# Causal attention scored on four row groups of the tensor engine, and layer norms that add their squares in halves before the variance matmul

## What is computed

```python
def _layernorm(x, axis=-1, eps=1e-05):
    m = jnp.mean(x, axis=axis, keepdims=True)
    v = jnp.var(x, axis=axis, keepdims=True)
    return (x - m) / jnp.sqrt(v + eps)
```

## Time and profile before

| | us |
|---|---|
| median of 3 runs | 2788.03 (2782.67 to 2789.25) |
| the profiled execution | 2787.26 |
| its span | 2785.5 |
| PE busy | 2124.0 (76%) |
| DVE busy | 1838.7 (66%) |
| ACT busy | 1340.7 (48%) |
| POOL busy | 1012.5 (36%) |
| mean granted TensorE clock | 0.896 |

### The profile page before, as it was taken

One profiled execution on the slowest core, in us unless ns is written; L12 is line 12 of the kernel. 1 busy time (PEld: TensorE's weight loads), 2 busy tenths in 40 slices (PEclk: granted clock), 3 DMA queues, 4 the chain that ended last, 5 costly groups with the idle time before them and its releaser, 6 DMA issues. The chain is left out here.

```text
span 2785.5 us, 34483 instructions
## 1 busy us (share of the span) xinstructions
PE 2124.0 (76%) x12315; PEld 1350.6 (48%) x12315; DVE 1838.7 (66%) x2425; ACT 1340.7 (48%) x2235; POOL 1012.5 (36%) x651
## 2 busy tenths in 40 slices
PE   2787666045698888988856999998896677689996
PEld 0455553012566666666634777775443233244442
DVE  4359883966677777777723554554353697899975
ACT  0013223552676677666632322323454685556655
POOL 1014532305246777777623333334110000443430
PEclk7998777576899999999968999999998898899998
DMA  3225555004448999999760000002132540000001
GB/s 137 60 97 193 192 196 201 0 0 137 166 154 245 260 255 249 255 261 257 181 234 0 1 1 0 0 0 106 46 113 83 204 152 1 0 1 1 1 1 61
DMA packets 123676, 313.50 MB, mean 113 GB/s; under 512 B 29569, under 2 KB 49537, under 8 KB 119810
## 3 DMA queue, kind: packets, MB, share of 16 engines
q1 hardware_dynamic: 102466, 260.69, 26.5%
q0 software_dynamic: 21056, 50.84, 9.2%
HBM read 219.59 MB, written 92.68 MB: 112 GB/s over the span
## 5 line engine op out<-in xcount | busy, mean ns | idle before, releaser
L1407 DVE SCALAR_TENSOR_TENSOR x_part<-x_group,x_scale,x_part 128x256 f32<-128x256 f32 x660 | 288.0, 477 | 144.7 <-ACT x_part L1349 136.9
L1296 PE MATMUL x_group<-x_xt,x_gu 128*128 128x256 f16 x2640 | 347.1, 275 | 1.8 <-DVE x_xt L1399 0.9
L1349 ACT ACTIVATE x_part<-x_group,x_scale 128x256 f32<-128x256 f32 x660 | 276.2, 471 | 123.1 <-PE x_group L1296 117.2
L1262 POOL TENSOR_TENSOR x_part<-x_part 128x512 f32<-128x512 f32 x165 | 235.3, 1430 | 197.2 <-DVE x_part L1407 197.2
L1296 PEld LDWEIGHTS x_group<-x_xt,x_gu 128*128 128x128 fp8e4 x2640 | 237.6, 98 | 85.7 <-issue 31.7
L1633 POOL TENSOR_TENSOR c_pt<-c_pt,const_tables 128x256 f32<-128x256 f32 x128 | 127.8, 1019 | 280.6 <-ACT c_pt L1741 280.3
L1313 PE MATMUL x_y_ps<-x_d_hi,x_h_hi 128*128 128x512 f32 x330 | 160.2, 485 | 68.8 <-DVE x_h_lo L1420 66.8
L2420 POOL TENSOR_TENSOR f_part<-f_part 128x1024 f32<-128x1024 f32 x44 | 120.4, 2735 | 187.9 <-DVE f_part L2447 187.9
L155 PE MATMUL mean_n<-residual,const_tables 128*128 128x512 f32 x160 | 80.0, 652 | 137.4 <-PEq L734 103.5
L2318 PE MATMUL f_group<-f_x_hi,f_raw 128*128 128x512 f16 x352 | 138.9, 395 | 32.3 <-DVE f_part L2447 24.9
L1253 POOL DMA_INDIRECT mixed_rows<-x_y,moe_rows x94 | 150.1, 1597 | 31.1 <-issue 20.8
(11 more groups left out here) (335 smaller groups left out, 5290.9 us busy)
## 6 DMA issues: line engine op xcount, KB each, us to landing
x_d_hi<-down_hi SPq DMA_DIRECT2D x50, 768.0 KB, 5.6
x_d_lo<-down_lo SPq DMA_DIRECT2D x50, 768.0 KB, 5.9
x_gu<-codes_gu SPq DMA_DIRECT2D x50, 384.0 KB, 5.8
p_w<-d_s SPq DMA_DIRECT2D x17, 768.0 KB, 7.5
down_hi<-p_hi SPq DMA_DIRECT2D x17, 768.0 KB, 3.9
down_lo<-p_lo SPq DMA_DIRECT2D x17, 768.0 KB, 6.2
aux<-ct SPq DMA_DIRECT2D x2, 4096.0 KB, 17.0
cross_values<-y_v_out SPq DMA_DIRECT2D x16, 512.0 KB, 3.0
```

The lines of the kernel that those rows point to most:

```text
L1262: pool.tensor_tensor(x[:, 0, :, :], x[:, 0, :, :], x[:, 1, :, :], ALU.add).then_inc(summed, 1)
L1296: mm = pe.matmul(group_ps[s % 2][:, q, :], codes[:, q, col:col + P], xt[u][:, k, q, :], start=k == 0, stop=k == 1)
L1349: act.activation(part[n % PARTS][:, q, o % 2, :], group_ps[s % 2][:, q, :], ACT.Copy, scale=scale[v][:, o, q:q + 1]).then_inc(ev_act, 1)
L1407: dve.scalar_tensor_tensor(x, group_ps[s % 2][:, 2 + q, :], scale[v][:, o, 2 + q:3 + q], x, ALU.mult, ALU.add).then_inc(ev_dve, 1)
```

## The change

**In the layer norm** VectorE gets a new step, `pair`: it adds chunks 2 and 3 of the squares onto chunks 0 and 1, in place. The variance then takes two matmuls a tile in place of four, and waits for `pair`. VectorE's queue is written out anew; TensorE's and ScalarE's keep their order.

**In the causal attention** q and k keep their layout and `spread` is gone: head j of a chunk lies on rows 32j to 32j+31, and the four heads of a chunk are scored by matmuls on four row groups, each into a PSUM bank of its own (`s_ps` takes four banks, and there is one of it). The 512 ** -0.5 moves into the exponential, which takes four heads at once (1536 columns), as does the mask; `pt` is a ring of three such groups. The squares of q and k are added on VectorE (`add_squares`) and summed by one matmul of 512 columns. The order of work is written out, without a loop, and the value projection reads the residual, not a copy of it.

```diff
             def var(t):
-                pe.wait_ge(squares_ready, base + t + 1)
+                pe.wait_ge(paired, base + t + 1)
                 if t >= 2:
                     pe.wait_ge(ln_ready, base + t - 1)
-                for c in range(C):
+                for c in range(C // 2):
                     mm = pe.matmul(var_ps[t % 2][:, :], g.const("mean"), squares[t % 2][:, c, :],
-                                   start=c == 0, stop=c == C - 1)
+                                   start=c == 0, stop=c == C // 2 - 1)
                 mm.then_inc(var_ready, 1)
 
             mean(0)
@@ -178,18 +177,36 @@
                 dve.tensor_tensor(centred[t][:, :, :], tile(src, t), bc(mean_ps[t % 2][:, :], 1, [P, C, TT]),
                                   ALU.subtract).then_inc(centred_ready, 1)
 
+            def pair(t):
+                dve.wait_ge(squares_ready, base + t + 1)
+                x = squares[t % 2]
+                dve.tensor_tensor(x[:, 0:2, :], x[:, 0:2, :], x[:, 2:4, :], ALU.add).then_inc(paired, 1)
+
+            def scale(t):
+                dve.wait_ge(rs_ready, base + t + 1)
+                dve.tensor_tensor(tile(dst, t), centred[t][:, :, :], bc(rs[t % 2][:, :], 1, [P, C, TT]),
+                                  ALU.mult).then_inc(normed, 1)
+
             if fill_vector is not None:
                 fill_vector(dve, 0)
             centre(0)
             centre(1)
-            for t in range(NT):
-                if t + 2 < NT:
-                    centre(t + 2)
-                if fill_vector is not None and t >= 1:
-                    fill_vector(dve, t)
-                dve.wait_ge(rs_ready, base + t + 1)
-                dve.tensor_tensor(tile(dst, t), centred[t][:, :, :], bc(rs[t % 2][:, :], 1, [P, C, TT]),
-                                  ALU.mult).then_inc(normed, 1)
+            pair(0)
+            centre(2)
+            pair(1)
+            if fill_vector is not None:
+                fill_vector(dve, 1)
+            scale(0)
+            centre(3)
+            pair(2)
+            if fill_vector is not None:
+                fill_vector(dve, 2)
+            scale(1)
+            pair(3)
+            if fill_vector is not None:
+                fill_vector(dve, 3)
+            scale(2)
+            scale(3)
 
         @block.scalar
...
-        xb = sb("xb", [P, C, S])
         q_raw, k_raw = sb("q_raw", [P, C, S]), sb("k_raw", [P, C, S])
-        sq, sk = sb("sq", [P, C, S]), sb("sk", [P, C, S])
+        squares = sb("squares", [P, 2, C, S])
+        pairs, sums = sb("pairs", [P, 2, 2, S]), sb("sums", [P, 2, S])
         nrm = sb("nrm", [P, 2, S])
-        q_sb = [sb(f"q{i}", [P, C, S]) for i in range(2)]
-        k_sb = sb("k", [P, C, S])
-        kp = [sb(f"kp{i}", [P, 4, S]) for i in range(2)]
-        v_sb = [sb(f"v{i}", [P, 2, D]) for i in range(2)]
-        pt = [sb(f"pt{i}", [P, 3, P]) for i in range(RING)]
-        at = [sb(f"at{i}", [P, C, S]) for i in range(2)]
-        out_ps, den_ps, work = ps("out_ps", [P, C, S]), ps("den_ps", [P, C, S]), ps("work", [P, C, S])
+        q_sb, k_sb = two("q", [P, C, S]), two("k", [P, C, S])
+        v_sb = two("v", [P, 2, D])
+        pt = [sb(f"pt{i}", [P, 4, 3, P]) for i in range(PT_RING)]
+        at = two("at", [P, C, S])
+        s_ps = ps("s", [P, 4, 4, P])
+        out_ps, den_ps = ps("out_ps", [P, 2, S]), ps("den_ps", [P, 2, S])
+        work = ps("work", [P, C, S])
         work_v = work[:, :, :].rearrange("p (k n) s -> p k (n s)", k=2)
-        s_ps = [ps(f"s{i}", [P, 3, P]) for i in range(2)]
...
-            def score(b, i, h):
-                c, j = h // 4, h % 4
-                if j == 0:
-                    pe.wait_ge(kp_ready, C * b + c + 1)
-                pe.wait_ge(exped, H1 * b + h + 1)
-                pe.matmul(s_ps[h % 2][:, 0:2, :], kp[c % 2][:, j, 0:P], q_sb[i][:, c, :], start=True, stop=True)
-                pe.matmul(s_ps[h % 2][:, 2, :], kp[c % 2][:, j, P:S], q_sb[i][:, c, P:S], start=True, stop=True)\
-                  .then_inc(s_done, 1)
...
+            def norms(b):
+                pe.wait_ge(v_read, b + 1)
+                pe.wait_ge(summed, b + 1)
+                pe.matmul(work[:, 2:4, :], g.const("ones"), sums[:, :, :], start=True, stop=True).then_inc(norm_done, 1)
+
...
+            def score(b, c):
+                n = GROUPS * b + c
+                if c == 0:
+                    pe.wait_ge(qk_ready, 2 * b + 2)
+                if n >= 1:
+                    pe.wait_ge(exped, n)
+                for k in range(2):
+                    for j in range(4):
+                        r = slice(32 * j, 32 * j + 32)
+                        out = s_ps[:, j, 0:2, :] if k == 0 else s_ps[:, j, 2, :]
+                        mm = pe.matmul(out, k_sb[b % 2][r, c, k * P:(k + 1) * P], q_sb[b % 2][r, c, k * P:S],
+                                       start=True, stop=True)
+                mm.then_inc(s_done, 1)
+
+            def values(b, c):
+                n, o = GROUPS * b + c, c % 2
+                pe.wait_ge(masked, n + 1)
+                if o == 0 and n >= 2:
+                    pe.wait_ge(divided, n // 2)
...
+                mm.then_inc(av_done, 1)
...
+            for b in range(-1, B):
+                now, following = b >= 0, b + 1 < B
+                if now:
+                    score(b, 0)
+                if following:
+                    queries(b + 1)
+                if b >= 1:
+                    values(b - 1, 3)
+                if now:
+                    score(b, 1)
+                if following:
+                    keys(b + 1)
+                if now:
+                    values(b, 0)
+                    score(b, 2)
+                if following:
+                    value_rows(b + 1)
+                if now:
+                    values(b, 1)
+                if following:
+                    norms(b + 1)
+                if now:
+                    score(b, 3)
+                if b >= 1:
+                    output(b - 1)
+                if now:
+                    values(b, 2)
...
+
+            def exponential(b, c):
+                n = GROUPS * b + c
+                act.wait_ge(s_done, n + 1)
+                if n >= PT_RING:
+                    act.wait_ge(av_done, n - PT_RING + 1)
+                act.activation(pt[n % PT_RING][:, :, :, :], s_ps[:, :, 0:3, :], ACT.Exp, scale=D ** -0.5).then_inc(exped, 1)
...
+            keep = g.const("causal").unsqueeze(1).unsqueeze(1).to_broadcast([P, 4, 2, P])
+            for n in range(GROUPS * B):
+                pool.wait_ge(exped, n + 1)
+                diagonal = pt[n % PT_RING][:, :, 0:3:2, :]
+                pool.tensor_tensor(diagonal, diagonal, keep, ALU.mult).then_inc(masked, 1)
 
...
-            def spread(b, c, first=False):
-
-                if not first:
-                    dve.wait_ge(s_done, H1 * b + 4 * (c - 1))
-                dve.tensor_tensor(kp[c % 2][:, :, :], bc(k_sb[:, c, :], 1, [P, 4, S]), bc(g.const("head4"), 2, [P, 4, S]),
-                                  ALU.mult).then_inc(kp_ready, 1)
...
+            def add_squares(b):
+                step(dve.tensor_tensor(pairs[:, :, :, :], squares[:, :, 0:2, :], squares[:, :, 2:4, :], ALU.add))
+                dve.tensor_tensor(sums[:, :, :], pairs[:, :, 0, :], pairs[:, :, 1, :], ALU.add).then_inc(summed, 1)
+
...
+            def divide(b, o):
+                pair = slice(2 * o, 2 * o + 2)
+                dve.wait_ge(av_done, GROUPS * b + 2 * o + 2)
+                if b >= 2:
+                    dve.wait_ge(o_done, b - 1)
+                step(dve.reciprocal(at[b % 2][:, pair, :], den_ps[:, :, :]))
+                dve.tensor_tensor(at[b % 2][:, pair, :], out_ps[:, :, :], at[b % 2][:, pair, :], ALU.mult)\
+                   .then_inc(divided, 1)
+
...
+            for b in range(-1, B):
+                now, following = b >= 0, b + 1 < B
+                if following:
+                    step(square(b + 1, 0))
+                if b >= 1:
+                    divide(b - 1, 1)
+                if following:
+                    step(square(b + 1, 1))
+                    add_squares(b + 1)
+                    value_rows(b + 1)
+                if now:
+                    divide(b, 0)
+                if following:
+                    normalise(b + 1)
+                if b >= 1:
+                    output(b - 1)
+            divide(B - 1, 1)
+            output(B - 1)
 
 
 
```

286 lines of the change are left out of this document (106 added, 180 removed).

## The result

The changed kernel takes 2755.75 us (median of 3 runs, 2751.54 to 2758.07), the kernel before 2788.03. The ratio is 0.9888 with a 95% interval of 0.9868 to 0.9908: 32 us faster, where 48 were forecast. TensorE is busy 2033.1 us (2124.0 before), VectorE 1842.1, ScalarE 1326.8, GpSimd 955.8; the mean granted clock is 0.884 (0.896 before).

The account below looks back on a forecast made before the run. It took the causal attention as bound by TensorE and a norm by a chain. From a span of 2785.5 us, -87 for the attention and +39 for six norms gave 2737.5, 2740 for the median; range 2710 to 2768.

Parts of the forecast that it names:

- the two halves: The change's two parts in the forecast: causal attention -87 us, six norms +39 us.
- A group at 0.65: Causal attention: four heads scored on overlapping row groups take 0.65 us, as one head did; 0.85 by the skill's speedup.
- A middle batch row at 39.2: Causal attention: TensorE's work 36.9 us, waits 1.8 and switches 0.5 make a batch row 39.2 us.
- Seven rows save 80: Causal attention: seven batch rows at 39.2 us each, in place of 354 us, save 80.
- The last row at 34: Causal attention's last batch row: exponential, mask and last division uncovered, 34 us in place of 40.6, saving 6.
- The start: Causal attention's first projections: still need each other's copies in turn, and save 1 us.
- The ring of a norm, +3.0: Layer norm: centre, pair, var, mean and steps form a ring of 8.9 us; a norm takes 41.0 for 38.0.
- The clock behind its gaps, +4: Layer norm: slow TensorE clock behind three idle gaps of 3.8 us costs 4 us a norm, between 0 and 5.1.
- Its rival, no slow clock: Layer norm: the clock does not fall in the gaps, norms cost 18 and the time is 2719 us; chance 0.17.
- The cross attention's norm, +8.5: Norm ahead of the cross attention: costs 8.5 us more, since its pairs meet GpSimd's split.
- Row groups without overlap: Causal attention scores: group 2.6 us, time 2789, chance 0.08; with weight-load waits too, 2800 to 2888, chance 0.04.
- VectorE's chain as the bound of the middle row: Causal attention: chain worse by GpSimd's longer masks, 2 us a batch row; with norms' upper end 2761 us; chance 0.05.

Follow-up runs that it names:

- wide scores: Changed kernel with each score group's second four matmuls taking 256 columns in place of 128: 2755.88 us.
- row 0 filled: 32 matmuls with overwritten result added in batch row 0, against the changed kernel with means ahead, GpSimd-side norms as before and last batch row reordered: 2689.49 us.
- the clock held up: Changed kernel with four matmuls of overwritten result ahead of each of a norm's first three waits for a pair: 2735.60 us.
- norms by eight: Changed kernel with the sums of squares of q and k from eight matmuls again, without VectorE's two additions: 2770.28 us.
- the mean ahead: Changed kernel with TensorE's queue reordered in the norm, mean(2) before var(0) and mean(3) before var(1): 2700.68 us.
- the two norms beside GpSimd left out: Against the kernel with the mean ahead, norms ahead of causal and cross attention take whole variances in the old order, without pairs: 2695.20 us.

## Why the prediction was right and where it was off

It was right in sign, in range and in its two main mechanisms, the overlap of the row groups and the ring in the norm. It was 16 us too low. Against the profiled execution, the two halves were off by 9 us each, the untouched stages lay 6 us the other way, which is luck, and the median lies 4 above this execution, where 1 was reckoned.

- **A group at 0.65.** Wrong by 0.22: the columns are 0.65, as the row of a single head had it, but the fixed price, of which 0.5 was entered once a batch row for changes of shape, falls due with each of its four groups, as 0.22. The upper figure that the prediction set beside it, 0.85, was the right one.
- **A middle batch row at 39.2.** It is 39.34, but by errors that cancel. TensorE's work was 38.7 and not 37.4 with the switches: groups 3.5 for 2.6, projections 28.4 for 27.6 (7.1 each, nearer the 7.0 to 7.2 of the earlier trace rows than the mean's 6.9). The waits were 0.65 for 1.8, since that work lies above VectorE's chain. The run with wide scores shows the exchange: half of the added work disappears in the wait.
- **Seven rows save 80.** They saved 74.7 (354.2 before, 279.5 after). This is the step that failed in the attention: the row in the middle was taken for all seven. Row 0 has no output projection above its 10.5 us of division and normalisation, waits 2.4 and 4.5 us, and hands row 1 a half clock. The run with row 0 filled shows both.
- **The last row at 34.** It took 38.1. Two divisions stood bare, where the working had one, and the work behind each was slow. The start saved 0.5 for 1. The mask, 2.8 and up to twice that, was 2.35 in the median and costs nothing, as forecast.
- **The ring of a norm, +3.0.** Right: TensorE idled 3.5 us three times, and with the clock held up a turn of the ring is 8.93 us for 8.9 and the norm ahead of the recurrence 41.03 for 41.0.
- **The clock behind its gaps, +4.** In the four norms without GpSimd it cost 5.9, 2.5, 1.1 and 5.9 us (with the first means in the first, 7.1): 3.9 in the mean, so the size was right and its ceiling of 5.1 was not. The working took the longest slow stretch from a row that shows only 3.4 us of one, 1.7 lost; behind the first gap here 2.9 were. Its rival, no slow clock, is refuted in the same rows.
- **The cross attention's norm, +8.5.** It cost 13.3, half of what the norms were over: this is the step that failed among them. Contention with GpSimd's split was entered with 1.5 us; the pairs waited 1.9 and 3.0, and the idle time ahead of var(0) and var(1) became 5.4 and 6.6.
- **Row groups without overlap**, both rivals: refuted by the group of 0.87. VectorE's chain as the bound of the middle row: refuted by the run of norms by eight.

What stays open is the scatter: the unchanged stages ahead of the first norm by up to 5 us between profiles, a norm of the same code without GpSimd by over 2, and those beside GpSimd by over 4 (50.4 to 54.9 ahead of the causal attention, 45.6 to 49.7 ahead of the cross attention).

## What to carry to other kernels

When a matmul is traded for work on another engine, ask first where the new result is waited for. The same pairs cost 48 us behind a mean that could have gone ahead, and gained some 9 (2709.9 to 2700.7) with the mean ahead and 15 with the two norms beside GpSimd left out. Cost the first and the last turn of a pipeline by themselves, since they lack the work that covers the others. And a gap on TensorE can end later than it seems: as an upper figure, add the half clock behind it, over as much work as the longest such stretch in the trace. Of the gaps of 3.5 us here one cost 2.9 us and another nothing.

## What the runs showed of the hardware that was not expected

- float32 matmuls on four row groups overlap whether or not their neighbours in the queue are on the same row group: 0.88 us a group head by head, 0.87 side by side. A group has a fixed price, 0.22 us with 384 columns a head and with 512 alike.
- More work on TensorE made a norm faster, 48.2 to 41.0 us: with gaps of 3.5 us filled its granted clock was 0.96 in place of 0.78. With the means ahead, where TensorE is not in the ring, a clock of 0.78 in place of 0.88 cost some 0.9 us (36.5 and 35.7).
- Beside GpSimd an addition with both inputs in SBUF ended 1.1 us after GpSimd's instruction did, five times out of five in the norm ahead of the cross attention (changed kernel and means ahead), while a subtraction with one input in PSUM kept its 2.29 us. It goes the other way too: where VectorE's scaling of two SBUF inputs had begun first (1855.68 to 1859.65 with the means ahead), GpSimd's product, else 4.5 us, took 6.45 and ended 4.38 after it.
